# First attention: values of two tiles in one block every second step, with new counts of the maxima and of GpSimd's tiles

## The reference, cut to what matters

```python
# 4 batches, 16 heads of 32 columns; x: 512 rows, cond: 1601 rows
q = _qdq(x) @ _qdq(wq).T + bq
k, v = jnp.split(cond @ wkv.T + bkv, 2, axis=-1)
attn = jax.nn.softmax(jnp.einsum('bnhd,bmhd->bhnm', q, k) * scale, axis=-1)
o = jnp.einsum('bhnm,bmhd->bnhd', attn, v).reshape(B, N, C)
```

## Time and profile before

| | |
|---|---|
| median of 3 runs | 2616.87 us (2613.92 to 2617.18) |
| profiled execution | 2618.84 us, span 2617.0 us |
| PE busy | 2524.9 us, 96% |
| DVE busy | 1786.3 us, 68% |
| GpSimd busy | 1294.0 us, 49% |
| ACT busy | 1231.3 us, 47% |

### The profile page before, as it was taken

The page is one execution under the profiler, slowest core; times in us unless marked ns, Lnnn a source line. Parts: engine busy times, 40 slices in busy tenths (PEclk is TensorE's granted clock), DMA queues, the critical chain, the costliest instruction groups (busy, mean ns, idle before and its releaser), DMA issues. The chain is left out here.

```text
span 2617.0 us, 33916 instructions
## 1 busy us (share of the span) xinstructions
PE 2524.9 (96%) x13272; PEld 1631.4 (62%) x13272; DVE 1786.3 (68%) x2457; ACT 1231.3 (47%) x1853; POOL 1294.0 (49%) x337
## 2 busy tenths in 40 slices
PE   8999999999999999999998999999899999998998
PEld 8888888887545545445444787787433333334786
DVE  5554554556767767777764666664799999998773
ACT  3221212311666666665664232322688888885110
POOL 0000000000999999999992000000499999997310
PEclk9999999999999999999999999999999999998999
DMA  8677676655535344354314754443997777776100
GB/s 298 231 241 244 239 274 242 212 168 160 110 80 116 71 95 105 67 110 90 68 65 149 242 173 156 150 153 102 247 190 164 166 166 167 158 195 204 57 33 33
DMA packets 218433, 405.11 MB, mean 155 GB/s; under 512 B 18168, under 2 KB 93976, under 8 KB 218208
## 3 DMA queue, kind: packets, MB, share of 16 engines
q1 hardware_dynamic: 218272, 402.93, 55.7%
HBM read 260.63 MB, written 140.59 MB: 153 GB/s over the span
## 5 line engine op out<-in xcount | busy, mean ns | idle before, releaser
L1378 POOL TENSOR_TENSOR pooled<-pooled,probs 128x2048 f32<-128x2048 f32 x140 | 640.7, 4577 | 21.0 <-POOL pooled L1378 0.9
L1225 ACT ACTIVATE probs<-psum 128x512 f32<-128x512 f32 (+1 forms) x832 | 458.4, 598 | 338.6 <-PE psum L1116 333.9
L1252 DVE TENSOR_REDUCE win_max<-psum 128x1 f32<-128x802 f32 x480 | 455.6, 988 | 151.0 <-PE psum L1081 150.6
L2127 DVE TENSOR_SCALAR probs<-psum,bound 128x1024 f32<-128x1024 f32 (+1 forms) x416 | 499.0, 1275 | 29.6 <-POOL pooled L2153 22.6
L2091 ACT ACTIVATE probs<-probs 128x1024 f32<-128x1024 f32 (+1 forms) x416 | 437.3, 1058 | 80.9 <-DVE probs L2127 39.0
L2153 POOL TENSOR_TENSOR pooled<-pooled,probs 128x2048 f32<-128x2048 f32 x94 | 433.2, 4608 | 13.1 <-ACT probs L2091 0.2
L1116 PE MATMUL psum<-q_st,k_st 128*128 128x512 f32 (+1 forms) x832 | 334.6, 439 | 18.4 <-ACT probs L1225 12.2
L261 POOL TENSOR_TENSOR r_q<-ve_q,minus_half 128x4 f32<-128x4 f32 x8 | 8.8, 1102 | 619.7 <-DVE ve_q L221 619.7
L1116 PEld LDWEIGHTS psum<-q_st,k_st 128*128 128x128 f32 (+1 forms) x832 | 149.4, 186 | 240.6 <-ACT probs L1225 179.2
L1081 PE MATMUL psum<-k_st,q_st 96*128 96x402 f32 x960 | 266.6, 359 | 6.3 <-DVE o_sb L1283 5.0
L2037 PE MATMUL psum<-q_st,k_st 128*128 128x512 f32 (+1 forms) x832 | 253.2, 430 | 16.3 <-DVE probs L2127 8.9
(11 more groups left out here) (265 smaller groups left out, 4233.0 us busy)
## 6 DMA issues: line engine op xcount, KB each, us to landing
k_st<-k_hi SPq DMA_DIRECT2D x64, 801.0 KB, 11.7
k_st<-k_lo SPq DMA_DIRECT2D x48, 801.0 KB, 11.2
k_hi<-kt_hi SPq DMA_DIRECT2D x32, 801.0 KB, 4.2
k_lo<-kt_lo SPq DMA_DIRECT2D x32, 801.0 KB, 6.1
v_rows<-v_out SPq DMA_DIRECT2D x96, 256.0 KB
v_st<-v_rows SPq DMA_DIRECT2D x24, 768.0 KB
q_st<-q_hi SPq DMA_DIRECT2D x64, 256.0 KB, 10.4
w<-w_hi_d SPq DMA_DIRECT2D x64, 256.0 KB, 3.1
```

Source lines behind the costliest of these rows:

```text
L1225: A.activation(probs[i % NPROBS][0:rows, j, :], bank(score_banks.where["score", u, t, j])[0:rows, :], ACT.Exp, scale=1.0 / ROOT).then_inc( ...
L1252: V.tensor_reduce(win_max[:, r, j, c:c + 1], window(windows.where["max", u, i])[:, :, 0:MV], AX.XY, ALU.max).then_inc(max_done, 1)
L1378: G.tensor_tensor(pooled[u % 2][:], before[:], probs[tile(u, k) % NPROBS][:], ALU.add).then_inc(pool_added, 1)
L2127: V.tensor_scalar(probs[i % NPROBS][0:rows, half * W:half * W + W, :], window(("score", u, t, half))[0:rows], bound[0:rows, u // NG, t:t + 1],
```

## The change

`VALUES` says in which step which tiles' values are made: tile 0 in step 2, tiles 1 and 2 in step 4, and so on, tiles 9 and 10 in step 12, and tiles 11 and 12 in step 1 of the next unit. Steps 0, 3, 5, 7, 9 and 11 have none. `WINDOWS` is a list now, with the number of windows of each step: two or four, 32 in all. In a step with four, PE's order is score 0, window, score 1, window, the values, window, score 2, window, score 3. In a step with two, it is score 0, window, score 1, the values if there are any, score 2, window, score 3. `LAST_SUM` becomes 2 and `CLOSE_AT` 5, so that `last_sum` and the copy of `den` stand in step 4 and the closing in step 5; the third score bank comes into use from step 6. `pooled_tiles` is 10 in odd units, so that GpSimd makes nine additions there and PE sums three tiles. ACT's program follows the same list.

```diff
@@ -989,8 +989,10 @@
         def attention_0(next_k, next_q, win_max, first, v_stored):
 
 
-            NQ, NSLOT, NPROBS, LAG, CLOSE_AT, TURN_AT, WINDOWS = 3, 3, 8, 2, 4, 11, 3
-            LAST_SUM, CODES_AT, ROWS_AT = 1, 3, 5
+            NQ, NSLOT, NPROBS, LAG, CLOSE_AT, TURN_AT = 3, 3, 8, 2, 5, 11
+            LAST_SUM, CODES_AT, ROWS_AT = 2, 3, 5
+            VALUES = {2: [0], 4: [1, 2], 6: [3, 4], 8: [5, 6], 10: [7, 8], 12: [9, 10], TT + 1: [11, 12]}
+            WINDOWS = [2, 4, 4, 2, 4, 2, 4, 2, 4, 2, 2, 0, 0]
             with ExitStack() as scope:
                 sbuf = allocator(scope)
                 sem, close = opened("b")
@@ -1037,7 +1039,7 @@
                     return (u - 1) * HPG * RT * 2 + i
 
                 def three_banks(u, t):
-                    return 5 <= t < pooled_tiles(u) + LAG
+                    return 6 <= t < pooled_tiles(u) + LAG
 
                 def window_of(i):
                     j, rest = divmod(i, RT * 2)
@@ -1045,11 +1047,11 @@
 
                 def windows_at(t):
 
-                    return range(min(t * WINDOWS, HPG * RT * 2), min((t + 1) * WINDOWS, HPG * RT * 2))
+                    return range(sum(WINDOWS[:t]), sum(WINDOWS[:t + 1]))
 
                 def pooled_tiles(u):
 
-                    return 11 if u < UNITS - 1 else 7
+                    return 11 - u % 2 if u < UNITS - 1 else 7
 
                 def kq_count(u):
 
@@ -1063,10 +1065,12 @@
                     return adds(u) + max(t, 1)
 
                 def steps():
+
                     for i in range(UNITS * TT + LAG):
                         u, t = divmod(i, TT)
-                        vu, vt = divmod(i - LAG, TT)
-                        yield (u, t) if u < UNITS else None, (vu, vt) if vu >= 0 else None
+                        behind = [(u - 1, v) for v in VALUES.get(t + TT, ()) if u]
+                        behind += [(u, v) for v in VALUES.get(t, ()) if u < UNITS]
+                        yield (u, t) if u < UNITS else None, behind
 
                 def pe_program():
                     def max_of(u, i):
@@ -1187,16 +1191,18 @@
                             max_of(*coming[0])
                         if now:
                             scores(*now, 1)
-                        if coming[1:]:
+                        if coming[2:]:
                             max_of(*coming[1])
-                        if behind:
-                            values(*behind)
-                            if behind[1] == LAST_SUM and behind[0]:
-                                last_sum(behind[0] - 1)
+                        for tile_behind in behind:
+                            values(*tile_behind)
+                            if tile_behind[1] == LAST_SUM and tile_behind[0]:
+                                last_sum(tile_behind[0] - 1)
+                        if coming[3:]:
+                            max_of(*coming[2])
                         if now:
                             scores(*now, 2)
-                        if coming[2:]:
-                            max_of(*coming[2])
+                        if coming[1:]:
+                            max_of(*coming[-1])
                         if now:
                             scores(*now, 3)
                             if now[1] == CLOSE_AT and now[0]:
@@ -1239,10 +1245,11 @@
                     for now, behind in steps():
                         if now:
                             exps(*now)
-                        if behind and behind[1] == TT - 1:
-                            copy_acc(behind[0])
-                        if behind and behind[1] == LAST_SUM and behind[0]:
-                            copy_den(behind[0] - 1)
+                        for vu, vt in behind:
+                            if vt == TT - 1:
+                                copy_acc(vu)
+                            if vt == LAST_SUM and vu:
+                                copy_den(vu - 1)
                     copy_den(UNITS - 1)
 
                 def dve_program():
```

## The result

The changed kernel takes 2633.26 us in the median of four runs (2631.15 to 2633.47), the kernel before 2615.55 (2613.92 to 2617.18, four runs). The ratio is 1.0066, 95% interval 1.0048 to 1.0083: slower by 17.7 us, with 2633 predicted. The profiled execution took 2633.47 us, its span is 2631.7, 14.7 longer than before.

The account below looks back on a forecast made before the run. PE's written order with its bank waits was taken as the bound. Units before the last +13.9, units 0 and 14 about -0.6, last unit +2.8: +16.1 us, giving 2633 by the median, range 2600 to 2646.

Parts of the forecast that it names:

- What bounds the kernel: First attention: PE's written order with its waits for PSUM banks sets the pace, GpSimd 0.7 us behind.
- 0.32 for each switch: PE entering and leaving a values block costs 0.32 us; 13 blocks becoming 7 saves 1.92 us per unit.
- the second window of the heavy step: Four-window steps 6 and 8: held by DVE's reductions, step 6 to 8 taking 6.85 us, old 7.03.
- The lost cover: Steps without values no longer give ACT and DVE 0.99 us to empty banks; units 48.02 even, 49.60 odd.
- walk: Each stretch between values blocks laid out by the trace's intervals; each could be off by about 0.1 us.
- The third score of the light step: Steps 3 and 5, without values: held for its bank, starting 1.19 us after the first score.
- The copy of `den`: On ACT before step 5's exponentials, uncovered, holding a score; step 4 to 6 takes 9.66 us, old 8.26.
- The last unit: First values to last sum: about 44.8 us against 42.0, +2.8, with no windows to fill the light steps.
- The sum: Whole kernel: +13.9 for units before the last, about -0.6 for units 0 and 14, +2.8 for the last; +16.1 us.
- the switches coming back in full: Rival A: exponentials and reductions ready in time, units of 46.35 us, 2595 us in all; 17%.
- rival C: Banks rotate badly at the unit's start, so even units lose what odd ones do: 2646 us; 7%.

Follow-up runs that it names:

- 9: As 8, but with nine GpSimd additions in odd units and bank 7 left to the scores to step 12: 2610.94 us, 0.9981 of the kernel before.
- experiment 4: Changed kernel with ACT's copy of den between the second and third exponential of step 4: 2627.25 us, 1.0043 of the kernel before.
- experiment 3: Changed kernel with values still in pairs but three windows a step, and ten additions in every unit: 2629.51 us, 1.0052 of the kernel before.
- Experiments 5: Kernel before with half the columns of exponentials, additions and reductions left out, PE's work uncut: 2579.7 us.
- experiment 6: Changed kernel with half the columns of exponentials, additions and reductions left out, PE's work uncut: 2577.1 us.
- experiments 1: Changed kernel with ten GpSimd additions in every unit: 2621.08 us, 1.002 of the kernel before.
- 2: Kernel before with only the nine GpSimd additions in odd units: 2622.15 us, 1.0024 of the kernel before.
- 7: Changed kernel with ten additions in every unit, the copy of den moved, last unit's values one tile a step: 2613.46 us, 0.9992 of the kernel before.
- 8: From 7, with values in pairs only where three score banks are in use, one tile a step elsewhere: 2605.18 us, 0.9958 of the kernel before.

## Why the prediction was right

- **What bounds the kernel.** PE's written order with its bank waits, GpSimd just behind it. Shown: nine additions made nothing faster, in either kernel or in 9.
- **0.32 for each switch.** It comes back in full with three banks (6.46 to 6.15 with short partners), and 0.20 of it with full ones (7.03 to 6.83), where the second window of the heavy step waits for DVE, as walked.
- **The lost cover.** Every stretch of the two units shown is within 0.10 us of its walk. The sum for a unit was 48.02 and 49.60, measured 47.88 and 49.52. The third score of the light step was to be held 1.19 after the first. In step 3 it is 1.27: the first score's exponential starts 0.62 after it and not 0.54, behind the one before. In step 5 (1145.36) the copy stands in front of it as well, and with the copy gone the hold is there still.
- **The copy of `den`.** It holds the score, as walked (9.66, measured 9.61). Taking it away gives 0.33: the loop behind it was already 0.3 late. The 0.6 that experiment 4 expected left that out, and not the walk.
- **The last unit.** +2.8 predicted, +4.8 measured, and most of the difference is a term that the prediction hasn't got, the clock (last section). In experiment 3 the last unit has the same instructions, and its stretches 8 to 10 and 10 to 12 have the clock at 1.00: they take 6.41 and 8.08 us where the new kernel takes 6.72 and 9.30. That is 1.5 of the 4.8; at full clock the unit would be 3.2 longer than the old one.
- **The sum.** The last unit's tile 0 comes 10.4 us later than before (1374.13 against 1363.70), where units 0 to 14 were to give 13.3: about 0.1 us too much in each, and a first block that stands 1.2 earlier. The last unit gives 2 more than its term. +16.1 stands against +14.7 in the span and +17.7 in the medians. The mechanism is as predicted, but that the sum came out this near is partly luck: two errors of nearly 2 us have opposite signs.
- **The rivals.** The nearest, the switches coming back in full, failed at the place it named: the third score of the light step is held. Experiments 5 and 6 show how far this is the partners' work: with half of it the score of step 3 is nearly free, but half of the 1.92 us still doesn't come back. That even units lose as much as odd ones (rival C) is not so, 47.88 against 49.52.

## What to carry to other kernels

Joining blocks on PE saves its switches and takes away the time in which its partners empty PSUM; lay the new order out instruction by instruction with the trace's own intervals, and join blocks only where there is a bank to spare (here three banks for four scores, not two). With two banks the loop of matmul, latency and eviction holds the step; halving the columns of the eviction took only 0.2 us off its 1.19. An engine that is 96% busy beside another is not the bound until taking work from it makes something faster: give it a trial of one line before building a schedule around its relief.

## What was not expected of the hardware

In the last unit of the new kernel, where light steps leave PE waiting (10.84 us busy of 12.00), the granted clock fell to 1.2 GHz of 2.4 for some 3 us, inside the block of four in step 10 (two stretches, columns as in the earlier trace rows):

```profile
1391.00:1403.00 12.00, 10.84 (x51) 3.86 (x49) 10.53 (x21) 8.20 (x16) 11.50 (x4) 1.00 0.01 2
1403.00:1406.00 3.00, 3.00 (x14) 0.88 (x17) 2.51 (x8) 1.37 (x3) 0.00 (x0) 0.51 0.00 0
```

The block took 4.79 us to the next score (1403.95 to 1408.74) where one of that length takes 3.57 at full clock (1403.47 to 1407.04 in experiment 3).

The new kernel isn't alone in this. The kernel of experiment 3 loses its clock in the last unit too, earlier, and step 4 to 6 takes 12.75 us there in place of 11.08:

```profile
1372.00:1385.00 13.00, 11.31 (x63) 5.04 (x63) 2.36 (x2) 8.30 (x17) 12.71 (x3) 1.00 0.00 1
1385.00:1391.64 6.64, 6.64 (x28) 3.73 (x27) 2.87 (x5) 1.04 (x3) 6.35 (x3) 0.74 0.13 39
1397.06:1411.55 14.49, 12.58 (x66) 4.08 (x65) 6.75 (x19) 8.90 (x18) 3.83 (x2) 1.00 0.00 1
```

The traces of experiments 1 and 4 have a fall in the last unit as well (granted 0.77 from 1403.45 to 1408.80 us and 0.73 from 1407.70 to 1413.34), the first of them another one just before it (0.79 from 1358 to 1366). These four kernels are those at full work with pairs in the last unit. The old kernel and those of experiments 2, 7, 8 and 9, with one tile a step there, have 1.00 throughout the last unit, and so has the short kernel of experiment 6, which has pairs. The place differs from trace to trace, and what decides it is open.
